# Moving expert 0's late entry from second to last place in a fused attention and mixture-of-experts kernel

## The reference

```python
x = x + jnp.tanh(g_xattn[0]) * attention(layernorm(x), ctx, ctx)   # 16 batches of 256 tokens, 32 query heads of 32
xf = layernorm(x).reshape(T, H)                                    # T = 4096 tokens, H = 1024
scores = jax.nn.softmax(xf @ w_cls.T, axis=-1)                     # 64 experts, of which 32 are real
_, topk_idx = jax.lax.top_k(scores + bias[None, :], 8)
w = scores at topk_idx; w = w / (w.sum(-1) + EPS) * 1.5
buf = the first 512 tokens of each real expert, in token order     # CAP = 512, the rest is dropped
g, u = jnp.split(buf @ w_gate_up, 2, axis=-1)                      # 1024 -> 2 x 512
y = (jax.nn.silu(g) * u) @ w_down                                  # 512 -> 1024
x = x + jnp.tanh(g_ffn[0]) * (w_routed-weighted sum of y per token) * (1 + w_zero.sum(-1))
```

## Time and profile before

| what | value |
|---|---|
| time, median of 3 runs | 2288.61 us (2286.43 to 2290.4) |
| the profiled execution, its own time | 2303.04 us |
| its span, first to last instruction | 2301.2 us |
| granted TensorE clock, mean | 0.982 of 2.4 GHz |
| instructions | 48610 |

### The profile page before, as it was taken

How to read it: one execution, slowest core, us unless ns; L and a number is a source line. 1 busy time by engine, 2 the same in 40 slices (tenths; PEclk the granted TensorE clock), 3 DMA queues, 4 the chain that set the end, 5 groups by cost and what they waited for, 6 DMA issues and landing times.

```text
span 2301.2 us, 48610 instructions
## 1 busy us (share of the span) xinstructions
PE 2114.8 (92%) x14776; PEld 1228.3 (53%) x14777; DVE 1453.7 (63%) x2463; ACT 1245.7 (54%) x1833; POOL 1072.1 (47%) x1241
## 2 busy tenths in 40 slices
PE   5999999989998596899999999999999999999996
PEld 2555554445554344456556564744656766454464
DVE  6788888888887564346446572833564865462383
ACT  3787777666775436235445463632553764353364
POOL 3127888877887465224322441622342643241262
PEclk9999999999999797999999999999999999999998
DMA  5567666657564656457666593955585986665582
GB/s 148 144 176 179 169 186 156 177 154 189 159 152 120 217 149 163 150 156 215 180 187 185 172 281 83 302 161 160 161 259 133 286 235 173 188 174 162 150 250 47
DMA packets 569277, 407.81 MB, mean 177 GB/s; under 512 B 213558, under 2 KB 489142, under 8 KB 569200
## 3 DMA queue, kind: packets, MB, share of 16 engines
q1 hardware_dynamic: 506112, 334.10, 50.1%
q0 software_dynamic: 46336, 72.10, 13.2%
q10 hardware_dynamic: 16752, 0.65, 0.5%
HBM read 319.33 MB, written 103.16 MB: 184 GB/s over the span
## 4 chain that ended last, share of the span: by engine, by line
PE 66%; DVE 14%; issue 9%; ACT 3%; POOL 3%; another core or an unknown queue 2%; DMA 1%; SPq 1%; DVEq 0%; POOLq 0%; ACTq 0%
PE psum L1673 35%; PE psum L1703 16%; DVE mx L1159 5%; PE psum L1560 5%; PE psum L1532 3%; PE psum L1545 2%; PE psum L1613 2%; DVE xgt L1328 1%; DVE stats L1124 1%; PE psum L1573 1%; DVE wgu L1316 1%; PE psum L1584 1%; DMA out_dram<-ys,slots 1%; PE psum L1509 1%
## 5 line engine op out<-in xcount | busy, mean ns | idle before, releaser
L1673 PE MATMUL psum<-xgt,wgu 128*128 128x256 f16 (+3 forms) x6336 | 907.0, 301 | 40.3 <-issue 25.1
L1673 PEld LDWEIGHTS psum<-xgt,wgu 128*128 (+1 forms) x6336 | 573.8, 98 | 372.7 <-issue 54.8
L807 POOL TENSOR_TENSOR spare<-spare 128x1 f32<-128x1 f32 x164 | 141.9, 865 | 856.1 <-PE psum L1703 432.5
L1703 PE MATMUL psum<-wdn,apair 128*128 128x512 f16 x1968 | 458.6, 384 | 19.1 <-issue 14.2
L1159 DVE TENSOR_REDUCE mx<-psum 128x2 f32<-128x512 f32 x512 | 327.3, 683 | 84.0 <-PE psum L1532 71.9
L1316 DVE SCALAR_TENSOR_TENSOR wgu<-wraw,wgu 128x1024 f16<-128x1024 f32 x264 | 318.4, 1216 | 41.2 <-ACT wgu L940 37.4
L724 POOL DMA_INDIRECT lists<-entry,dest x256 | 268.4, 1049 | 114.3 <-issue 69.7
L923 ACT ACTIVATE prob<-psum 128x512 f32<-128x512 f32 x512 | 277.3, 598 | 72.1 <-PE psum L1545 38.6
L1338 DVE SCALAR_TENSOR_TENSOR a<-psum,sg 128x512 f32<-128x512 f32 x132 | 91.0, 689 | 350.2 <-PE psum L1673 335.9
L1328 DVE COPY xgt<-psum 128x1024 f16<-128x1024 f16 x256 | 167.0, 682 | 225.0 <-PE psum L1613 206.4
L1703 PEld LDWEIGHTS psum<-wdn,apair 128*128 128x128 f16 x1968 | 187.9, 99 | 223.7 <-issue 30.4
(11 more groups left out here) (157 smaller groups left out, 1943.5 us busy)
## 6 DMA issues: line engine op xcount, KB each, us to landing
wraw<-in_L_ffn_w_gate_up_dram SPq DMA_DIRECT2D x264, 512.0 KB
wraw<-in_L_ffn_w_down_dram SPq DMA_DIRECT2D x132, 512.0 KB
x<-in_x_dram SPq DMA_DIRECT2D x16, 1024.0 KB
xr<-in_x_dram SPq DMA_DIRECT2D x16, 1024.0 KB
out_dram<-x SPq DMA_DIRECT2D x16, 1024.0 KB
pairs<-xs SPq DMA_DIRECT2D x16, 1024.0 KB
qs<-qh SPq DMA_DIRECT2D x248, 64.0 KB
qs<-ql SPq DMA_DIRECT2D x128, 64.0 KB
```

The source lines that it names most:

```text
L1673: mm = pe.matmul(ps_gu[:, s, h, 0:nt * P], w[:, a, k, :], xgt[:, c, k, 0:nt * P], start=(k == 0 and (a, c) == (0, 0)), stop=(k == KB - 1 a ...
L1703: mm = pe.matmul(psum[:, Y_BANK[i] + n2, :], apair[:, o, k, c * P:(c + 1) * P], w[:, a, k, :], start=(k == 0 and (a, o) == (0, 0)), stop=( ...
```

## The change

The late entry of expert 0 becomes entry 32, and experts 1 to 31 become entries 1 to 31. Expert 0's pairs of the last batches have no scatters of their own any more. Since entry 1 is now expert 1, its list needs all scatters of all batches. `counts(14)`, `logits(15)` and `counts(15)` stand one half of `up` earlier in entry 0. `closing(0)` no longer mixes matmuls and `t_rows`, and DVE copies the `t_rows` of entry 1. In steps 15 and 16 the scatters of batches 12 and 13 are spread over the slots in another way. With LAST ten of batch 12's sixteen scatters stand in step 15 and six in step 16; before, all sixteen stood in step 15.

```diff
         def weights_of(e):
 
-            return 0 if is_first(e) else e - 1
+            return 0 if isinstance(e, int) and e in (0, nq - 1) else e
...
                     for half_out in lists_out:
-                        sp.wait_ge(half_out, 8 * T2 * TOPK * (nb - 2))
-                    sp.wait_ge(first_out, 2 * 16 * T2)
+                        sp.wait_ge(half_out, 8 * T2 * TOPK * nb)
                     get_gslots(1, 1)
                     sp.dma_start(slots[:, 1], lists_v[1]).then_inc(slots_in[1], 16)
-                    for half_out in lists_out:
-                        sp.wait_ge(half_out, 8 * T2 * TOPK * nb)
                     get_gslots(2, 0)
...
-            const(pool.iota(slot0[:], pattern=[[CAP, NROUTED]], base=CAP - int(NO_SLOT), channel_multiplier=0,
+            const(pool.iota(slot0[:], pattern=[[CAP, NROUTED]], base=-int(NO_SLOT), channel_multiplier=0,
...
-            def scatter_first(b):
-                pool.wait_ge(first_ready, b - nb + 3)
...
             LATE = (0, 0, 3, 3, 3, 3, 4, 0)
+            LAST = (0, 0, 0, 2, 2, 3, 3, 0)
...
+                    if kv < 2 and at_step(b, nb):
+                        scatter(b - 4, par, 10 + 3 * kv, 13 + 3 * kv, 8 * b + kv - 2)
...
-                            scatter(b - 3, 1 - par, 9 * (kv - 2), 9 if kv == 2 else T2 * TOPK)
+                    if at_step(b, nb) and kv in (2, 3):
+                        scatter(b - 3, 1 - par, 5 * (kv - 2), 5 if kv == 2 else T2 * TOPK)
+                    elif early(b) and kv == 3:
+                        scatter(b - 3, 1 - par, 0, T2 * TOPK)
...
-            scatter(nb - 2, nb % 2, 12, T2 * TOPK)
             gather(1, 1)
-            scatter(nb - 1, 1 - nb % 2, 0, T2 * TOPK)
...
-                        if is_first(e) and (i, n2) in TAKES:
-                            take_second(TAKES.index((i, n2)))
...
-                    tally.add(dve.tensor_scalar(slot0[:, 0:1], carry[:, 0:1], -1.0, float(CAP) - NO_SLOT, ALU.mult, ALU.add))
+                    tally.add(dve.tensor_scalar(slot0[:, 0:1], carry[:, 0:1], -1.0, float(NROUTED * CAP) - NO_SLOT, ALU.mult, ALU.add))
...
-            def first_entries(b, tally):
...
                 if is_first(e):
-                    for h in range(6):
+                    for h in range(4):
                         gu_lo(1, h // 2, h % 2)
+                    for u in range(8):
+                        take_t(1, u)
+                    for h in range(2):
+                        gu_lo(1, 2, h)
                     return
...
+                    if (j, h) == (0, 1):
+                        counts(nb - 2)
                     if (j, h) == (1, 0):
-                        counts(nb - 2)
-                    if (j, h) == (1, 1):
                         logits(nb - 1)
-                    if (j, h) == (2, 1):
+                    if (j, h) == (2, 0):
                         counts(nb - 1)
...
-                if not last:
+                if not last and not is_first(e):
                     for u in (0, 1):
                         t_rows(e + 1, u)
...
                 mm.then_inc(y_full, 1)
+                if is_first(e):
+                    for u in range(4):
+                        t_rows(1, u)
```

More of the change, by code:

```diff
@@ L374, in on_pool @@
             return not (isinstance(b, int) and b >= nb - 3)
-        def apart(b):
-            return isinstance(b, int) and b >= nb - 2
         def is_first(b):
@@ L782, in step @@
                         factors(b - 2)
-                    if at_step(b, nb):
-                        if kv in (2, 3):
-                            scatter(b - 3, 1 - par, 9 * (kv - 2), 9 if kv == 2 else T2 * TOPK)
-                    elif at_step(b, nb + 1):
-                        if kv == 3:
-                            scatter_first(b - 3)
-                            scatter(b - 3, 1 - par, 0, 12)
-                    elif early(b):
-                        if kv == 3:
-                            scatter_first(b - 3)
-                    elif kv >= 2 and on(b, -3):
-                        share = LATE if at_step(b, nb - 1) or at_step(b, nb - 2) else SHARE
+                    if at_step(b, nb) and kv in (2, 3):
+                        scatter(b - 3, 1 - par, 5 * (kv - 2), 5 if kv == 2 else T2 * TOPK)
+                    elif early(b) and kv == 3:
+                        scatter(b - 3, 1 - par, 0, T2 * TOPK)
+                    elif not early(b) and kv >= 2 and on(b, -3):
+                        share = LAST if at_step(b, nb - 1) else LATE if at_step(b, nb - 2) else SHARE
                         first = sum(share[:kv])
@@ L1031, in _ @@
             loops(act, step, mybir.EngineType.Activation)
-            TAKES = ((0, 0), (0, 1), (1, 1), (2, 1))
-            def take_second(u):
-                c, part = u // 2, u % 2
-                act.wait_ge(gt_full, 8 + u + 1)
-                act.activation(xgt[:, part, :, c * P:(c + 1) * P],
-                               ps_g16[u % 2].rearrange("p (k t) -> p k t", k=KB), ACT.Copy).then_inc(gt_free, 1)
             def get_slots(e, par):
@@ L1070, in step2 @@
                     for n2 in range(2):
-                        if is_first(e) and (i, n2) == (CT - 1, 1):
-                            for u in range(4, 8):
-                                take_second(u)
                         y_out(e, par, i, n2)
-                        if is_first(e) and (i, n2) in TAKES:
-                            take_second(TAKES.index((i, n2)))
                         if i == 0 and not last:
@@ L1262, in positions @@
                     tally.wait()
-            def first_entries(b, tally):
-                dve.wait_ge(list_ready, b + 1)
-                tally.wait()
-                link(dve.tensor_tensor(spot0[:, b % 2], place[:, :, 0], mask[:, :, 0], ALU.mult), tally)
-                tally.add(dve.tensor_scalar(dest0[:, b % 2], spot0[:, b % 2], NO_SLOT, None, ALU.add))
-                tally.add(dve.tensor_copy(entry0[:, b % 2, :, 1].bitcast(F32), coef[:, :, 0]))
-                link(dve.tensor_copy(entry0[:, b % 2, :, 0], token[:, :, 0]), tally)
-                dve.memset(place[:, :, 0:1], 0.0).then_inc(first_ready, 1)
             def entries_a(b, tally):
                 dve.wait_ge(list_ready, b + 1)
-                if apart(b):
-                    dve.wait_ge(first_ready, b - nb + 3)
                 if not on_pool(b - 1):
@@ L1386, in step @@
                         positions(b - 2, tally)
-                        if apart(b - 2):
-                            first_entries(b - 2, tally)
                     if kv == 7 and at_step(b, nb + 1):
@@ L1752, in closing @@
                     mm = down_part(0, 0, k)
-                    if not last and k < 2:
+                    if not last and not is_first(e) and k < 2:
                         t_rows(e + 1, 2 + k)
                 mm.then_inc(y_full, 1)
+                if is_first(e):
+                    for u in range(4):
+                        t_rows(1, u)
             def opening(e, nt):
```

17 lines of the change are left out of this document (3 added, 14 removed).

## The result

The kernel after took 2291.09 us, median of 20 runs (2287.92 to 2293.05); the kernel before 2287.44 us beside it (20 runs, 2283.20 to 2290.95). The ratio is 1.0016, with an interval of [1.0009, 1.0022]: 3.7 us slower, where I had forecast 8.5 us faster. It is inside my range and within the 0.2% that I called no change, but on the other side of 1.

What follows compares the result with a forecast made beforehand. PE, busy 92% of the span, was taken as the bound, so time is won only where it stands still or does needless work. Front -26.8 and end +18.3 sum to -8.5 us: 2288.6 to 2280.1, range 2268 to 2293.

Steps and rivals of the forecast that it cites:

- The front's term: Entry 0 to expert 1: `up` of expert 1 starts at 908.5 and not 935.28, 26.8 us earlier.
- 18.3: End of the kernel, net: 24.2 - 9.5 + 7 + 1.5 - 4.9 = +18.3 us for the empty entry run last.
- wait and slow matmuls that go: Expert 31, now in the loop: its 6.9 us code wait and 2.6 us of slow matmuls go, 9.5 us.
- The front's steps: Entry 0 to expert 1: scatters end 869.9, rows there 886.3, PE waits 14.7, `t_rows` 4, cold code 10.6, opening 7.6 us.
- rival 3: Ahead of expert 1: gather late behind weight loads and scatters, rows at 895, no gain, 2285 to 2291 us; chance 0.18.
- The dealing at nothing: Steps 15 and 16: the new spread of batch 12 and 13's scatters costs nothing.
- Its cover: Step 16, ahead of `rstd(15)`: POOL's 7.39 us wait for DVE hides the two added scatters, 2.8 us.
- Rival 2: First entries of three, two and one block meet cold code, 10 to 22 us: 2291 to 2302 us; chance 0.12.
- The end: Empty last entry: +24.2 us of work, +7 and +1.5 for cold code, -4.9 for a shorter tail.
- the tail: Behind PE's end: an empty add moves nothing, so 5.6 us and not 10.5, -4.9.
- the load and the slow opening: Last entry's one-block body, cold: one code load and a slow opening, +7 us (bounds 3.5 and 9.5).
- the jump to its closing: Last entry: far jump to its `closing`, +1.5 us, part of which hides behind the split of the weights.

Runs made afterwards that it cites:

- b_again: The kernel before, unchanged, profiled once more on chip A (first kind): 2288.06 us, ratio 1.0003; its profiled execution took 2288.72 us.
- a_half: The kernel after with only 8 of the 16 scatters of batch 15, chip B: 2284.55 us, against 2297.89 for the kernel after there.
- a_four: The kernel after with an entry's four bodies laid out in code as 4, 3, 2, 1 blocks, chip B: 2282.59 us, ratio 0.9883.
- a_rot: The kernel after with PE's loop turned by half an entry, so the last body runs from loop code, chip B: 2294.56 us.
- a_rot4: The kernel after with PE's loop turned by half an entry and bodies in the order 4, 3, 2, 1, chip B: 2277.67 us, ratio 0.9866.
- b_again3: The kernel before, unchanged, on chip D (second kind), beside the run without batch 15's scatters: 2305.88 us.
- a_again: The kernel after, unchanged, on chip B (second kind): 2297.89 us, ratio 0.9952 against the kernel before.

## Why the prediction was wrong

**The step that failed** is this one: "That execution was 14.4 us above the median; where, the trace alone doesn't tell. The parts of my sum are differences of stages of the same kind, so I take them over." The front's term was not such a difference. Its side "after" I built from single durations; its side "before" was the distance 802.53 to 935.28 on the trace, 132.8 us, and 10.8 of them were fits of PE, and waits of PE for a late ACT, that this execution had and those of the first kind of chip have not. With b_again's trace the same distance is 121.0 us, and my own working gives 121.04 - 105.97 = 15.1 us in place of 26.8, and a sum of -15.1 + 18.3 = +3.2 us. The timing said +3.7. That these two are so close is partly luck, as other errors cancel: the front after was 2.6 us shorter than forecast, the end 3.7 longer. The term that failed is the -26.8; it measured -17.7, 11.7 us less for the side before and 2.6 more for the side after.

**Term by term**, in us, the kernel after against b_again, both on the first kind by their times:

| | forecast | traces |
|---|---|---|
| start of `up` of entry 0 | 0 | -0.6 |
| `up` of entry 0 to `up` of expert 1 | -26.8 | 121.0 to 103.4: -17.7 |
| to `up` of expert 31 (wait and slow matmuls that go) | -9.5 | 1323.4 to 1313.6: -9.8 |
| to the last instruction | +27.8 | 43.1 to 74.5: +31.5 |
| sum | -8.5 | +3.5 |

**The front's steps** held. Counted from `up` of entry 0, the last scatter ended at 68.4 (67.4 forecast) and the rows were there at 83.8 (83.8). The exact hit is luck: the scatters began 1.9 us early and took 2.9 longer, their first one alone 4.78 us, and the gather landed 11.1 us after its start, where I had 12.4. The wait is 3.1 us longer than forecast because PE was done earlier, not because the rows came late; rival 3 is out. a_half shows that the wait is for the scatters, a_four that the 8.5 us behind it are cold code, where I had 10.6.

**The dealing at nothing** was right on the first kind, by two kernels. Its cover had shrunk as I had worked out: POOL waited 7.39 us for DVE ahead of `rstd` before, and 0.73 now. One scatter more there would have been on the path.

**Rival 2**, cold code of the other three bodies, is out: from `up` of expert 1 to `up` of expert 9 the two kernels take 379.2 us each, and PE has no "issue" wait of 1 us or more there in the kernel after. For jumps of this length the rule of the Trainium skill, "Runtime: NRT & Kernel Launch", section "Instruction fetch mechanics", that a taken branch outside the window waits for a load, fits what a_four shows: 8.78 us and three loaded blocks ahead of the body that comes last, 0.42 us and none ahead of the one that comes first.

**The end** was 3.7 us too cheap: the tail by 1.9, the rest in the last entry. For the load and the slow opening I had 7; they cost 2.73 us and 1.8 (12 matmuls in 4.45 and not 2.67). For the jump to its closing I had 1.5; PE waits 3.67 us there, and 24 matmuls take 8.22 us and not 5.34. Not all of that wait is code: the profile names ACT's `ys` as what ended it, and with PE's code in another order (a_four, a_rot, a_rot4) 1.8 to 2.0 us are left. This wait for ACT wasn't in my sum.

**So where did the gain go?** The late entry at the second place cost 49.3 us, but it stood over the scatters of batch 15, the gather behind them and a jump, for which PE now waits 17.8 + 8.5 us. Taking it away was worth 17.7 us, less than the 21.7 (31.5 - 9.8) that it costs at the end, where nothing lies behind it. On the second kind it was worth 21.7 (134.8 in b_again3 on D to 113.1 in a_again on B) against 18.0. Why it is worth more there is open. It isn't that the scatters of batch 15 now run while PE waits: in a_again they run from 852.1 to 877.3, and PE works on down blocks from 856.4 to 876.1, 84 matmuls in 19.77 us and not 18.29. The same 16 scatters beside the mixed `t_rows` and matmuls of the kernel before go with 12.4 us. Which code is hurt, and by what, no run here separates.

**What stays open.** Why two kinds of chip differ, whether it is the chip and not some other state of the machine (four chips were seen, B in two groups), what it is in POOL's scatters that reaches PE and ACT, and the rest of the 20 us. The traces of a_again (B) and b_again3 (D) account for 4.6 of the 9.9 us that the change wins on the second kind; 3.4 more is how far the profiled execution of a_again lay above its median. That the first profile was made on a chip of the second kind isn't on record. I argue it from the lengths of its intervals and from its 11 "remote" waits, of which no trace of the first kind has one.

## What to carry to other kernels

When a profiled execution lies well off the median of the timed ones, find where before a difference is taken from it: a side built from durations and a side read as a distance on the trace don't share the excess. Rows with "issue" between matmuls of one block, at a place where the same code elsewhere has none, are the mark, and so are "remote" waits of the other engines in a program on one core. Empty work beside a wait is cheap; price its removal by what it covers, and look first at the cold jumps next to it: two edits that only order PE's code (the body that comes first, first in the code; the last entry run from the loop) won 18 to 20 us on top of the change under study, with the kernel after taken from another chip of the same kind for the 18.

## What the runs showed of the hardware

- The same kernel took 2288 us on two chips and 2306 to 2308 on two others, and one change was 0.16% slower on the first kind and 0.48% faster on the second.
- On the second kind PE's code between 840 and 890 us came in fits of one to some matmuls, 0.7 or 1.4 us apart, while POOL issued scatters of 128 small pairs; without 16 of them 11.2 us came back (D), on a chip of the first kind 2.8 (C). ACT and DVE stood still too: ACT's first copy began 3.2 to 4.1 us after the `t_rows` that it copies (b_again3, first profile), 0.65 us after them in b_again.
- A jump of PE to a body not yet run that lies behind three others cost 8.4 to 8.9 us (6.8 in a_rot), with three or four 16 KB blocks loaded; to the one right behind the jump 0.4 us, with none.
